# Layer 1's head sums on TensorE and the mixer's row scalings on ScalarE, with a new order of steps, in a four-layer network

## Time and profile before

| | |
|---|---|
| median of 3 runs | 3212.63 us |
| profiled execution, span of its instructions | 3209.0 us |
| time around the span (median minus span) | 3.6 us |
| VectorE (DVE) busy | 2544.2 us, 79% |
| TensorE (PE) busy | 2383.4 us, 74% |
| ScalarE (ACT) busy | 1633.2 us, 51% |
| mean granted TensorE clock | 0.860 of full |
| layers012 | about 0 to 1950 us |
| layer 3's attention | about 2296 to 3116 us |

### The profile page before, as it was taken

How to read it: one execution, slowest core, us unless ns; L and a number is a source line. 1 busy time by engine, 2 the same in 40 slices (tenths; PEclk the granted TensorE clock), 3 DMA queues, 4 the chain that set the end, 5 groups by cost and what they waited for, 6 DMA issues and landing times.

```text
span 3209.0 us, 40003 instructions
## 1 busy us (share of the span) xinstructions
PE 2383.4 (74%) x13729; PEld 1300.2 (41%) x13729; DVE 2544.2 (79%) x5554; ACT 1633.2 (51%) x3182; POOL 565.8 (18%) x610
## 2 busy tenths in 40 slices
PE   3697876967958769679674304997688898888888
PEld 1333333333333333334331101332366676666663
DVE  3386898998999999989989673887577777777764
ACT  1344436245344353353442412666587888777862
POOL 0000300302203003012030020001332323323320
PEclk9698987977978879779777655999799999999999
DMA  2001100100101001001010004200688877888751
GB/s 73 1 22 43 30 25 28 35 32 23 34 29 30 26 24 33 28 27 31 30 24 23 23 8 123 57 9 31 198 226 223 235 222 225 220 215 227 220 157 43
DMA packets 270758, 265.92 MB, mean 83 GB/s; under 512 B 15224, under 2 KB 244235, under 8 KB 268987
## 3 DMA queue, kind: packets, MB, share of 16 engines
q1 hardware_dynamic: 270554, 263.37, 28.8%
HBM read 130.48 MB, written 124.45 MB: 79 GB/s over the span
## 4 chain that ended last, share of the span: by engine, by line
DVE 41%; PE 31%; ACT 14%; issue 9%; DMA 2%; POOL 2%; SPq 1%; DVEq 0%; POOLq 0%; ACTq 0%
PE banks L2642 5%; PE banks L2688 4%; DVE t L2618 3%; DVE t L1017 2%; PE banks L2602 2%; DVE t L1169 2%; ACT L144 2%; DVE t L952 1%; ACT t L2629 1%; PE banks L1085 1%; ACT t L2553 1%; DVE t L2673 1%; DVE t L1700 1%; DVE t L1704 1%; ACT t L1395 1%
## 5 line engine op out<-in xcount | busy, mean ns | idle before, releaser
L2618 DVE CUSTOM_DVE_ANT_0 t<-banks,t 128x640 f32<-128x640 f32 (+7 forms) x512 | 377.8, 747 | 135.2 <-PE banks L2642 62.2
L2629 ACT ACTIVATE t<-t 128x640 f32<-128x640 f32 (+7 forms) x512 | 391.0, 780 | 81.3 <-DVE t L2618 80.4
L2642 PE MATMUL banks<-ident,t 128*128 128x128 f32 x2304 | 360.1, 281 | 41.6 <-DVE t L2839 14.4
L2642 PEld LDWEIGHTS banks<-ident,t 128*128 128x128 f32 x2304 | 253.8, 142 | 108.1 <-ACT t L2629 50.5
L2602 PE MATMUL banks<-t 128*128 128x512 bf16 (+3 forms) x768 | 197.3, 333 | 39.4 <-DVE t L2618 37.5
L2583 POOL TENSOR_TENSOR t<-t 128x512 f32<-128x512 f32 x96 | 122.6, 1277 | 551.1 <-DMA t<-relative_scratch 455.7
L548 POOL TENSOR_TENSOR t<-t 128x512 f32<-128x512 f32 x28 | 48.1, 1718 | 915.7 <-ACT t L520 915.7
L2673 DVE COPY t<-banks 128x512 f32<-128x512 f32 x256 | 175.6, 686 | 32.2 <-PE banks L2642 31.3
L1085 PE MATMUL banks<-t 128*128 128x512 f32 x256 | 145.0, 650 | 42.9 <-DVE t L1165 32.3
L1740 ACT ACTIVATE t<-t 128x16 f32<-128x16 f32 x256 | 82.5, 322 | 184.1 <-DVE t L1704 142.4
L1119 ACT ACTIVATE t<-banks 128x512 f32<-128x512 f32 x128 | 76.4, 597 | 195.6 <-PE banks L1085 195.4
(11 more groups left out here) (453 smaller groups left out, 5956.2 us busy)
## 6 DMA issues: line engine op xcount, KB each, us to landing
relative_scratch<-t SPq DMA_DIRECT2D x128, 512.0 KB, 3.6
t<-relative_scratch SPq DMA_DIRECT2D x128, 512.0 KB, 5.2
relative_scratch<-t SPq DMA_DIRECT2D x128, 256.0 KB, 4.1
t<-in_wmoe SPq DMA_DIRECT2D x64, 384.0 KB, 3.0
t<-cut_scratch SPq DMA_DIRECT2D x192, 64.0 KB
t<-t SPq DMA_DIRECT2D x16, 512.0 KB, 4.2
cut_scratch<-t SPq DMA_DIRECT2D x8, 768.0 KB, 4.1
z_scratch<-t SPq DMA_DIRECT2D x8, 512.0 KB, 3.1
```

What stands on the lines that cost most here:

```text
L2618: nc.vector.tensor_tensor_reduce(s.s[z][:, 0:n], ps[:, b0:b0 + 1 + i // 4, :].rearrange("p b n -> p (b n)")[:, 0:n], s.bias[r][:, j, WIDE ...
L2629: nc.scalar.activation(s.s[z][:, 0:n], s.s[z][:, 0:n], ACT.Exp, scale=-1.0, bias=s.least[:, z:z + 1]).then_inc(*a.mark("weights", u))
L2642: nc.tensor.transpose(ps[:, 4 + c % 2, (t - lo) * P:(t - lo + 1) * P], s.s[u % NS][:, t * P:(t + 1) * P], k.ident[:]).then_inc(*e.mark("tu ...
```

## The change

- Layer 1's sums: DVE's product is laid out with the summed index outermost, and PE sums it by accumulating matmuls with the identity: 8 matmuls of 256 columns per tile for the scores (L914 of the changed kernel), 16 of 128 columns per tile for the output (L923), which come out transposed, so that the transposes go. DVE's two reduces go. ScalarE copies the scores from PSUM (L940). Two product buffers take turns; the second shares its place with the cumulative sums. The weights' columns are arranged to suit.
- Banks: `heads` holds banks 3 and 4 until the scores are copied, not only until qkv is.
- Mixer: xdt, xdd and the old state's scaling become 4 ScalarE copies each (one per head, 64 columns, scale by a column of numbers, L510, L528, L534) instead of one DVE instruction each; DVE adds the scaled state `kept` to the new one (L633). y's matmuls wait for DVE's `low` (L622) and ScalarE's `xdd`.
- Order: all TURNS strings but POOL's are new, those of `outputs2` and `attention3` too. ScalarE's queue now holds 108 table loads, before 94.

```diff
@@ -446,8 +446,8 @@
         for h in range(H0):
             o = ps[(h % 2) * HP:(h % 2 + 1) * HP, h // 2, (3 - 2 * (h // 2)) * P:(4 - 2 * (h // 2)) * P]
             yield
-            pe.wait_ge(v, "xdd", u, t)
-            pe.wait_ge(a, "btok", u, t)
+            pe.wait_ge(v, "gated_low", u, t)
+            pe.wait_ge(a, "xdd", u, t)
             mm(o, s.xdt[:, h, :], s.low[:, h, :], start=True, stop=first).then_inc(*e.mark())
             if not first:
                 yield
@@ -503,8 +503,12 @@
     nc.scalar.activation(s.t16[:], s.t16[:], ACT.Ln, bias=k.one[:]).then_inc(*a.mark("softplus", u))
     for t in range(NT):
         yield
-        act.wait_ge(v, "xdt", u, t)
+        act.wait_ge(e, "turned", u, t)
         nc.scalar.copy(s.btok[:], ps[:, 0, DI0:DI0 + P]).then_inc(*a.mark("btok", u, t))
+        yield
+        for h in range(H0):
+            nc.scalar.activation(s.xdt[:, h, :], ps[:, 0, h * HP:(h + 1) * HP], ACT.Copy, scale=s.dt[:, t, h:h + 1]).then_inc(
+                *a.mark("xdt", u, t))
         yield
         act.wait_ge(v, "low", u, t)
         for h in range(H0):
@@ -518,6 +522,17 @@
         nc.scalar.activation(s.low, s.low, ACT.Exp, scale=-1.0).then_inc(*a.mark())
         k.table(LOGEXP)
         nc.scalar.activation(s.dd[:], s.dd[:], ACT.Exp).then_inc(*a.mark("decay", u, t))
+        yield
+        act.wait_ge(a)
+        for h in range(H0):
+            nc.scalar.activation(s.xdd[:, h, :], s.xdt[:, h, :], ACT.Copy, scale=s.dd[:, h:h + 1]).then_inc(*a.mark("xdd", u, t))
+        if u:
+            yield
+            if t:
+                act.wait_ge(v, "state", u, t - 1)
+            for h in range(H0):
+                nc.scalar.activation(s.kept[:, h, :], s.state[:, t, h, :], ACT.Copy, scale=s.ec[:, h, P - 1:P]).then_inc(
+                    *a.mark("kept", u, t))
     for j in range(2):
         yield
         act.wait_ge(e, "z", u, j)
@@ -595,9 +610,6 @@
     for t in range(NT):
         ct = slice(t * P, (t + 1) * P)
         yield
-        dve.wait_ge(e, "turned", u, t)
-        tt(s.xdt[:], ps[:, 0, 0:DI0].rearrange("p (h q) -> p h q", h=H0), rep(s.dt[:, t, :], 2, HP), ALU.mult).then_inc(*v.mark("xdt", u, t))
-        yield
         dve.wait_ge(e, "rows", u, t)
         rows = bank(ps, 2).rearrange("p (h t) -> p h t", h=H0)
         copy(s.acs[:], ps[:, 1, DI0:DI0 + H0]).then_inc(*v.mark())
@@ -607,8 +619,7 @@
         tt(s.dd[:], rows[:, :, P - 1], s.acs[:], ALU.subtract).then_inc(*v.mark("low", u, t))
         yield
         dve.wait_ge(a, "decay", u, t)
-        tt(s.low, s.low, rep(s.gm[:], 1, H0), ALU.mult).then_inc(*v.mark())
-        tt(s.xdd[:], s.xdt[:], rep(s.dd[:], 2, HP), ALU.mult).then_inc(*v.mark("xdd", u, t))
+        tt(s.low, s.low, rep(s.gm[:], 1, H0), ALU.mult).then_inc(*v.mark("gated_low", u, t))
         yield
         dve.wait_ge(e, "y", u, t)
         for c in range(2):
@@ -618,10 +629,8 @@
         if first:
             copy(s.state[:, t], new).then_inc(*v.mark("state", u, t))
         else:
-            tt(s.state[:, t], s.state[:, t], rep(s.ec[:, :, P - 1], 2, HP), ALU.mult).then_inc(*v.mark())
-            yield
-            dve.wait_ge(v)
-            tt(s.state[:, t], s.state[:, t], new, ALU.add).then_inc(*v.mark("state", u, t))
+            dve.wait_ge(a, "kept", u, t)
+            tt(s.state[:, t], s.kept[:], new, ALU.add).then_inc(*v.mark("state", u, t))
     yield
     dve.wait_ge(a, "z", u, 1)
     dve.wait_ge(v)
@@ -845,7 +854,7 @@
     nc, dve, v, loads = k.nc, k.dve, k.line("w1_dve"), k.queue("w1_loads")
     dve.wait_ge(loads, "all")
     for j in range(3):
-        nc.vector.tensor_tensor(s.wqkv[:, j * D:(j + 1) * D], s.wqkv[:, j * D:(j + 1) * D], blocks[:, j // 2], ALU.mult).then_inc(
+        nc.vector.tensor_tensor(s.wqkv[:, j * D:(j + 1) * D], s.wqkv[:, j * D:(j + 1) * D], blocks[:, j % 2], ALU.mult).then_inc(
             *v.mark("all"))
 
 
@@ -863,12 +872,16 @@
 def att1_views(take):
     o = Bag()
     o.qkv = take((NT, 3 * D))
-    o.z, o.cum, o.cumsq = (take((NT, NH * NH)) for _ in range(3))
-    o.s_tok, o.masked = (o.cum.rearrange("p t g -> p (t g)")[:, 0:TB].rearrange("p (t d) -> p t d", t=NT) for _ in range(2))
-    o.prod = take((2 * NT * NH * NH,))
-    o.sa, o.sb = (o.prod[:, i * NT * NH * NH:(i + 1) * NT * NH * NH].rearrange("p (t g) -> p t g", t=NT) for i in range(2))
+    o.z, sums = take((NT, NH * NH)), take((2 * NT * NH * NH,))
+    o.cum, o.cumsq = (sums[:, i * NT * NH * NH:(i + 1) * NT * NH * NH].rearrange("p (t g) -> p t g", t=NT) for i in range(2))
+    o.masked = o.cum.rearrange("p t g -> p (t g)")[:, 0:TB].rearrange("p (t d) -> p t d", t=NT)
+    o.prod = [take((2 * NT * NH * NH,)), sums[:, 0:2 * NT * NH * NH]]
+    o.sa, o.sb = (o.prod[0][:, i * NT * NH * NH:(i + 1) * NT * NH * NH].rearrange("p (t g) -> p t g", t=NT) for i in range(2))
     o.one, o.star, o.tau = take((NT * NH,)), take((NT * NH,)), o.sb
     return o
+
+
+SOME = 4
 
 
 def att1_pe(k, s, u, free):
@@ -890,11 +903,25 @@
         mm(bank(ps, bk, 3 * D), x, s.wqkv[:], start=True, stop=False).then_inc(*e.mark())
         mm(bank(ps, bk, 3 * D), s.ones[0:1], s.bias[0:1, 0:3 * D], start=False, stop=True).then_inc(*e.mark("qkv", u, t))
     for t in range(NT):
-        yield
-        for line, *key in free("heads_out", u):
-            pe.wait_ge(line, *key)
-        pe.wait_ge(v, "s_tok", u, t)
-        nc.tensor.transpose(ps[:, bk, t * P:(t + 1) * P], o.s_tok[:, t], k.ident[:]).then_inc(*e.mark("s_tok", u))
+        for d in range(HD):
+            if d % SOME == 0:
+                yield
+                pe.wait_ge(v, "products", u, t)
+                if t >= 2:
+                    pe.wait_ge(a, "z", u, t - 2)
+                elif t:
+                    pe.wait_ge(a, "qkv", u, NT - 1)
+            mm(bank(ps, bk + (t + 1) % 2, NH * NH), k.ident[:], o.prod[t % 2][:, d * NH * NH:(d + 1) * NH * NH], start=(d == 0),
+               stop=(d == HD - 1)).then_inc(*e.mark("z", u, t))
+    for t in range(NT):
+        for g in range(NH):
+            if g % SOME == 0:
+                yield
+                for line, *key in free("heads_out", u):
+                    pe.wait_ge(line, *key)
+                pe.wait_ge(v, "valued", u, t)
+            mm(ps[:, bk, t * P:(t + 1) * P], o.prod[t % 2][:, g * D:(g + 1) * D], k.ident[:], start=(g == 0), stop=(g == NH - 1)).then_inc(
+                *e.mark("s_T", u, t))
 
 
 def att1_act(k, s, u):
@@ -904,9 +931,13 @@
         yield
         act.wait_ge(e, "qkv", u, t)
         if u:
-            act.wait_ge(v, "s_tok", u - 1, NT - 1)
+            act.wait_ge(v, "valued", u - 1, NT - 1)
         nc.scalar.activation(o.qkv[:, t, 0:D], bank(ps, bk, D), ACT.Copy, scale=ATTN_SCALE1).then_inc(*a.mark())
         nc.scalar.copy(o.qkv[:, t, D:], ps[:, bk, D:3 * D]).then_inc(*a.mark("qkv", u, t))
+    for t in range(NT):
+        yield
+        act.wait_ge(e, "z", u, t)
+        nc.scalar.copy(o.z[:, t], bank(ps, bk + (t + 1) % 2, NH * NH)).then_inc(*a.mark("z", u, t))
     yield
     act.wait_ge(v, "sorted", u)
     nc.scalar.activation(o.sb, o.sa, ACT.Square).then_inc(*a.mark("squares", u))
@@ -925,7 +956,7 @@
     act.wait_ge(a)
     nc.scalar.activation(o.z, o.z, ACT.Square).then_inc(*a.mark("weights", u))
     yield
-    act.wait_ge(e, "s_tok", u)
+    act.wait_ge(e, "s_T", u, NT - 1)
     if u:
         act.wait_ge(v, "x", u - 1)
     nc.scalar.copy(s.s_T[:], bank(ps, bk)).then_inc(*a.mark("s_T", u))
@@ -935,25 +966,26 @@
     nc, dve, (e, a, v), o = k.nc, k.dve, att1_lines(k), s.att
     tt, ts, reduce, copy = nc.vector.tensor_tensor, nc.vector.tensor_scalar, nc.vector.tensor_reduce, nc.vector.tensor_copy
     rows = NT * NH
-    prod = o.prod
     if u == 0:
         yield
         dve.wait_ge(k.line("norm1_dve"), "xn", u)
         tt(o.masked, s.xn1[:].rearrange("p (t n) -> p t n", t=NT), rep(s.before[:], 1, NT), ALU.mult).then_inc(*v.mark("masked", u))
-    yield
-    if u:
-        dve.wait_ge(a, "weights", u - 1)
     for t in range(NT):
-        q = o.qkv[:, t, 0:D].rearrange("p (h d) -> p h d", h=NH)
-        kk = o.qkv[:, t, D:2 * D].rearrange("p (h d) -> p h d", h=NH)
+        q = o.qkv[:, t, 0:D].rearrange("p (h d) -> p d h", h=NH)
+        kk = o.qkv[:, t, D:2 * D].rearrange("p (d g) -> p d g", g=NH)
         yield
         dve.wait_ge(a, "qkv", u, t)
         dve.wait_ge(v)
-        tt(prod.rearrange("p (h g d) -> p h g d", h=NH, g=NH), rep(q, 2, NH), rep(kk, 1, NH), ALU.mult).then_inc(*v.mark())
-        yield
-        dve.wait_ge(v)
-        reduce(o.z[:, t], prod.rearrange("p (x d) -> p x d", d=HD), AX, ALU.add).then_inc(*v.mark())
-    yield
+        if t >= 2:
+            dve.wait_ge(e, "z", u, t - 2)
+        elif u:
+            dve.wait_ge(e, "s_T", u - 1, t + 2)
+        else:
+            dve.wait_ge(e, "qkv", u, NT - 1)
+        tt(o.prod[t % 2].rearrange("p (d h g) -> p d h g", h=NH, g=NH), rep(q, 3, NH), rep(kk, 2, NH), ALU.mult).then_inc(
+            *v.mark("products", u, t))
+    yield
```

(24 more changed lines are left out.)

198 lines of the change are left out of this document (100 added, 98 removed).

## The result

The changed kernel is slower: 3317.6 us (median of 4 runs, 3307.7 to 3325.0) against 3220.1 us for the kernel before on the same chip (4 runs, 3210.4 to 3227.8; the time before given above is the median of three of these four). The ratio is 1.031, with a 95% interval from 1.027 to 1.035. The forecast was 3080 us, and its range ended at 3165. The profiled execution has a span of 3318.9 us, 109.9 more than the 3209.0 of before.

What follows compares the result with a forecast made beforehand. DVE was taken to set the rounds, with PE coming level: 19 us less a round, 133 over seven, perhaps 5 at the ends, against 5 for attention, gave -133 and a median of 3080 us. Its range: 3045 to 3115; overall 2998 to 3165.

Steps and rivals of the forecast that it cites:

- The reduces and the scalings: DVE: reduces, xdt, state scaling and xdd's own work go, 183.8 us, 23.3 a full round; products cost the same.
- The stall of L611: Mixer's xdd on DVE, held up beside GpSimd: 26.6 us of stall pass to the next such instruction, none won.
- PE's added work: PE's summing matmuls: +27 us a round at full clock, giving 163, or 178 at a clock of 0.92.
- ScalarE: Small copies at 0.27 us and 14 more table loads: some 16 us a round on top of 92, hidden.
- PE waits no longer than before: Mixer tile's chain: four ScalarE copies, at most 1.15 us, replace L611's 1.48 behind the decay, so PE's wait does not grow.
- The sum: DVE's idle grows from 12.6 to about 17 us a round; round 196.6 us, 19 less; median 3080.
- Start and end: First and last units' parts outside the seven rounds: perhaps 5 us gained.
- Rival 2: PE becomes the bound if its clock stays at 0.83: rounds of 206 to 207 us, 3147 us; chance 0.20.
- Rival 3: Layer 3's attention loses as transfers start some 2.4 us later at 16 places: 38 us, 3118 us; chance 0.07.
- Rival 4: `heads` holding banks 3 and 4 longer sets the rounds, about 5 us longer each: 3253 us; chance 0.08.
- Rivals 1: DVE's cut converts in full and the stall disappears too: 210 us gained, 3002 us; chance 0.12.
- rival 5: Half-clock sums on PE eat the cut, nothing to be told apart: about 3205 us; chance 0.05.

Runs made afterwards that it cites:

- e8: Changed kernel's arithmetic, first three layers' order laid out anew allowing for GpSimd/VectorE blocking, later stages' tables of the kernel before: 3165.0 us, ratio 0.983.
- e5: Changed kernel with only the first three layers' order strings laid out anew from traced durations, GpSimd blocking not considered: 3237.4 us, ratio 1.007.
- e11: Changed kernel with layer 1's sums as DVE reduces, mixer's copies kept on ScalarE, order laid out as in e8: 3157.0 us, ratio 0.980.
- e4: Changed kernel's new order with layer 1's sums and the mixer's scalings both back on DVE: 3409.9 us, ratio 1.062 to the kernel before.
- e1: Changed kernel with only every fourth of the matmuls that sum layer 1's products: 3298.9 us, ratio 1.027 to the kernel before.
- e7: Changed kernel with the order tables of outputs2 and attention3 put back to those of the kernel before: 3297.9 us, ratio 1.026.
- e9: Arithmetic of the kernel before, first three layers' order laid out as in e8, later stages as before: 3238.8 us, ratio 1.005.

## Why the prediction was wrong

- **The reduces and the scalings: right.** The durations of DVE's instructions fell by 22.7 us a round, forecast 23.3. Its busy time fell to 189.0 only, where the forecast had 179.6, as the instructions overlap less with gaps between them; in e8, with the same work, it is 182.0. The products kept their price in the new layout: L985 has a mean of 2392 ns, L952 had 2386.
- **The stall of L611: right in kind.** It was taken as kept, by the rule of the Trainium skill that two such instructions shut each other out ("SBUF — State Buffer", section "Who interferes with whom"). L622 now takes 815 ns in the mean; the same instruction took 0.69 us before. That is some 4 us in all, so most of the 26.6 us of stall left this place; that none of it was won for DVE as a whole fits the 22.7 us above. The rule's other side, that GpSimd is shut out as well, was left out of the sum: 0.45 us against 2.44 in the rows above. In the changed kernel it made DVE wait 9.1 us in five rounds, in e5 58.8.
- **PE's added work: right.** 183.5 us at a clock of 0.88 is 161 us of full clock, forecast 163; in e8 178.2 us at 0.90, forecast 178 at 0.92.
- **ScalarE: the total right, the place wrong.** It rose by 16.2 us a round (92.0 to 108.2), forecast 16. The price held: a single copy reads 323 to 340 ns, but four in a train take about 1.06 us, 0.265 each, where the forecast had 0.27 and at most 1.15 for four. The Trainium skill has a rule ("ScalarE: Activation LUTs", section "Rules for kernel authors") of about 0.3 us and 0.83 ns per element for an ACTIVATE with its bias by pointer. For 64 elements that is an estimate of 0.35 us; here it is the scale that comes by pointer, and the rows of single copies agree within 0.03 us. The sentence "PE waits no longer than before" fell all the same: 60.9 us became 69.4, and 76.4 in e8. It was not the copies' length, as at 979 us the train ends 1.14 us after the mark `decay` (L524's end), where L611 in the earlier trace rows ended 2.1 us after its mark (L520's end); in e11, with the same copies, PE waits 30.5 us.
- **The sum: this step failed.** "I expect DVE's idle time to grow from 12.6 to about 17 us a round" took the new order to be as tight as the old one, and it was the one large thing for which no row was read. It is 36.2 us. The round is 28.6 us longer than forecast: 19.2 of idle time and 9.4 of busy time, nearly all of it overlap that was lost. e4 shows by itself what the order can cost, 190 us, where the forecast charged 31 for more idle time (seven rounds of 4.4) and 5 for the attention; e8 shows 152.6 with the changed arithmetic. Even in e8's order the idle time was 24.6 and the round 206.6, so 10 of the 19 us forecast as a round's gain did not come.
- **Start and end.** The first and last unit were to give 5 us; the first gave 39 away, again by the order, since e4 has it too (its second unit begins 57 us later than before) and e8, with the same work, has 7 of it.
- **Rival 2, PE as the bound (3147).** In part: PE has 51% of the chain, and is full at half clock in places. But e1, with a quarter of the sums, saves 19 us only, and e8 is fast with all of them. The load alone is not the bound.
- **Rival 3, attention (3118).** Right in direction. The attention lost 9.9 us, outputs2 13.5, and putting the old tables back gave 19.7 (e7); the price of 38 was too high.
- **Rival 4, shared banks (3253).** Its sign was right, and the idle time of 36 us at which it was to decide has come about. Its mechanism was not: e4 has the earlier release of the banks and is slower still, and e8 has the later one and is fast.
- **Rivals 1 (3002) and 5 (3205).** DVE's cut was never converted in full, not even in e8; and the end lay far above rival 5's.

Along the path over e4, the medians give 189.9 us lost by the order and 92.3 won by the arithmetic, 97.5 in all. What stays open is which moves in the strings cost most, as no single engine's string was put back alone, and whether an order exists in which both halves add up.

## What to carry to other kernels

When a change rewrites the order of a program in which two engines are about three quarters busy (79% and 74% here), cost the order as a change of its own: run the old arithmetic in the new order first. Take the idle time of the leading engine from nothing but the order that will run; here it was 36 or 25 us a round with the same work (the change, e8), and 30 or 17 with that of before (e4, e9). And lay it out with the stretched durations, TensorE's at half clock and GpSimd's beside VectorE's long products, as a chain that looks slack at its usual price is not so where single steps of it take five times theirs: it cost e5 58.8 us of waits in five rounds. Count an engine's work by the durations of its instructions as well as by its busy time, which here fell by 13.5 us a round where the durations fell by 22.7.

## What the runs showed of the hardware

- A GpSimd instruction of 0.45 us (L1637, L1638) takes 2.44 to 2.56 us if it starts while VectorE is in a 2.3 us product of two SBUF operands; in the rows above it ended 0.3 to 0.5 us after that product. VectorE loses up to 0.44 us on such a long product (L985, 2278 to 2714 ns), and up to 1.1 us on a short one that starts behind a GpSimd product (L622, 670 to 1761 ns).
- PE can be fully busy at half clock: it is never idle from 1066 to 1071 us of the changed kernel, at a granted clock of 0.50. In e1, fewer matmuls in the same waits brought the clock of five rounds from 0.88 down to 0.83.
- A ScalarE copy of 64 columns with a number per row reads 323 to 340 ns, from PSUM or from SBUF, in the mean, and four in a train take 0.92 to 1.07 us.
- VectorE instructions that follow without a gap overlap: 1122.3 us of durations stood in 1012.6 us of busy time before, and 1121.8 in 1051.8 in e4, with more gaps.
